# A four-stage transformer block on one core: how layers hand over, two orders changed, the output in parts

## The reference

```python
x = x + 0.5 * L0_ffn(layernorm(x))    # 8 experts, top 2, for each of gate, up, down
x = x + L0_attn(layernorm(x))         # 16 heads of 8; weights polymax(s), no softmax
x = x + 0.5 * L0_ffn(layernorm(x))
x = x + 0.5 * L1_ffn(layernorm(x))    # 128 -> 512 -> 128, gelu; weights of each batch element
x = x + L1_attn(layernorm(x))         # 16 heads on one latent of 36; softmax
x = x + 0.5 * L1_ffn(layernorm(x))
```

## Time and profile before

| what | us |
| --- | --- |
| median of 3 executions (lowest, highest) | 3112.09 (3107.85, 3112.73) |
| the profiled execution, its own time | 3102.54 |
| its span | 3100.8 |
| TensorE busy | 2719.5 (88 %) |
| VectorE busy | 2029.5 (65 %) |
| ScalarE busy | 1148.7 (37 %) |
| GpSimd busy | 884.5 (29 %) |
| landing of the 2 MB output | 8.7 |
| landing of an 8 KB row of maxima | 1.8 |
| landing of a 256 KB weight issued among many others | 5.4 |

### The profile page before, as it was taken

How to read it: one execution, slowest core, us unless ns; L and a number is a source line. 1 busy time by engine, 2 the same in 40 slices (tenths; PEclk the granted TensorE clock), 3 DMA queues, 4 the chain that set the end, 5 groups by cost and what they waited for, 6 DMA issues and landing times. The chain is left out here.

```text
span 3100.8 us, 53905 instructions
## 1 busy us (share of the span) xinstructions
PE 2719.5 (88%) x15208; PEld 1879.4 (61%) x15208; DVE 2029.5 (65%) x5166; ACT 1148.7 (37%) x2097; POOL 884.5 (29%) x1200
## 2 busy tenths in 40 slices
PE   6999999958787888789999999768988989889986
PEld 5888888735454555468888887334554554454453
DVE  6777777747776777577777777445555555556533
ACT  3111111126575657521111111324544535545532
POOL 3333223225555555442233222001211111111200
PEclk9999999968888888889999999878999999999988
DMA  3000000000000000020000000000101101101100
GB/s 134 0 0 0 0 0 0 1 1 3 3 2 3 3 3 2 17 84 0 0 0 0 0 0 0 1 23 27 45 24 35 37 25 36 36 24 38 34 1 27
DMA packets 31864, 52.01 MB, mean 17 GB/s; under 512 B 8066, under 2 KB 13954, under 8 KB 31620
## 3 DMA queue, kind: packets, MB, share of 16 engines
q1 hardware_dynamic: 27012, 41.88, 4.3%
q0 software_dynamic: 4608, 7.09, 0.9%
HBM read 17.93 MB, written 2.10 MB: 6 GB/s over the span
## 5 line engine op out<-in xcount | busy, mean ns | idle before, releaser
L603 DVE SCALAR_TENSOR_TENSOR moe_acc<-moe_ps,moe_comb,moe_acc 128x512 f32<-128x512 f32 x896 | 660.4, 743 | 153.1 <-PE moe_ps L310 146.8
L2149 DVE CUSTOM_DVE_ANT_0 attn_masked<-attn_psm,attn_causal 128x256 f32<-128x256 f32 (+7 forms) x512 | 368.6, 756 | 271.3 <-PE attn_psm L1846 270.3
L2051 ACT ACTIVATE attn_probs<-attn_pse 128x512 f32<-128x512 f32 (+1 forms) x640 | 313.2, 556 | 324.9 <-PE attn_pse L1861 322.2
L310 PE MATMUL moe_ps<-moe_Wg,moe_xh 128*128 128x512 f32 x1024 | 328.1, 402 | 17.4 <-DVE moe_Wg L526 17.4
L341 PE MATMUL moe_ps<-moe_Wd,moe_ih 128*128 128x512 f32 x1024 | 339.3, 413 | 4.7 <-DVE moe_Wd L526 4.7
L310 PE MATMUL moe_ps<-moe_Wu,moe_xh 128*128 128x512 f32 x1024 | 332.0, 406 | 3.5 <-POOL moe_Wu L464 3.5
L1769 POOL TENSOR_SCALAR_AFFINE_SELECT attn_probs<-attn_probs 128x256 f32<-128x256 f32 (+1 forms) x192 | 95.0, 495 | 726.3 <-ACT attn_probs L2051 726.3
L1877 PE MATMUL attn_psy<-attn_probs,attn_V 128*64 128x512 f32 (+3 forms) x1536 | 288.7, 506 | 0.0
L474 POOL TENSOR_SCALAR moe_part<-consts,moe_pick,moe_prob 128x8 f32<-128x8 f32 x256 | 97.4, 394 | 626.0 <-ACT moe_prob L398 626.0
L1077 POOL TENSOR_TENSOR attn_R<-attn_R 128x1024 f32<-128x1024 f32 (+1 forms) x128 | 215.0, 1687 | 200.2 <-DVE attn_R L1421 200.1
L1846 PE MATMUL attn_psm<-attn_kS,attn_qS 108*128 108x512 f32 (+3 forms) x672 | 199.0, 397 | 45.7 <-DVE attn_mx L2149 39.7
(11 more groups left out here) (218 smaller groups left out, 4802.5 us busy)
## 6 DMA issues: line engine op xcount, KB each, us to landing
attn_qS<-attn_qH SPq DMA_DIRECT2D x192, 72.0 KB
attn_qS<-attn_qL SPq DMA_DIRECT2D x96, 72.0 KB
attn_qS<-attn_qH POOLq DMA_DIRECT2D x64, 72.0 KB, 2.0
moe_stageg<-in_w_gate SPq DMA_DIRECT2D x8, 512.0 KB, 7.1
moe_stageu<-in_w_up SPq DMA_DIRECT2D x8, 512.0 KB, 7.2
moe_stageg<-in_w_down SPq DMA_DIRECT2D x8, 512.0 KB, 4.4
attn_qS<-attn_qL POOLq DMA_DIRECT2D x32, 72.0 KB, 2.5
out<-X SPq DMA_DIRECT2D x1, 2048.0 KB, 8.7
```

The source lines that it names most:

```text
L310: last = pe.matmul(expert_bank[j % 4][:, :], a[q][:, :], w[b][:, cols], start=k == 0, stop=k == 2)
L603: dve.scalar_tensor_tensor(acc[:, q, r, :], expert_bank[j % 4][:, :], comb[:, q, r, e:e + 1], acc[:, q, r, :], ALU.mult, ALU.add).then_inc ...
L2051: act.activation(probs[:, ring(q, u), c, HALF - n:HALF], e_part(k, HALF - n, HALF), ACT.Exp, scale=SCORE_SCALE).then_inc(p_ready, 1)
L2149: dve.tensor_tensor_reduce(masked[:, 0 if j >= 4 else 1, 0:n], m_all[:, base:base + n], causal[:, SEQ - n:SEQ], 1.0, NEG, ALU.add, ALU.max ...
```

## The change

Semaphores of a phase are cleared by SyncE within the next one (`clear_spent`), behind SyncE's own first or last work there, and no block of their own is left; the last phase's are cleared in `end_phase`. An activation on one element asks for a table ahead of time: square root at the end of four phases and, without a switch, of polynomial attention (`load_sqrt`), gelu ahead of the feed-forward loop, exp ahead of latent attention's. `ffn_phase` can get an output; it then adds into X at once, without statistics, and SyncE sends X out by 4 tiles of tokens as each half is done. The orders in the two attentions change as the pieces below show.

```diff
+    def clear_spent(self, sp):
+        if self.spent:
+            for s in self.spent.all:
+                sp.sem_clear(s)
...
@@ ffn_phase, SyncE
+                def store(b):
+                    for s in range(2):
+                        n = b * BT + 4 * s
+                        sp.wait_ge(res.xo_ready, after(b * 2 + s))
+                        sp.dma_start(out.rearrange("(n p) c -> p n c", p=P)[:, n:n + 4, :], t.X[:, n:n + 4, :]).then_inc(out_done, 16)
+                rows(0)
+                sem.clear_spent(sp)
+                for b in range(BATCH):
+                    if b + 1 < BATCH:
+                        rows(b + 1)
+                    if out is not None:
+                        store(b)
@@ ffn_phase, ScalarE
                 layernorm_scales(act, t, rstd_ready)
+                act.activation(t.warm[:, :], t.consts[:, 0:1], ACT.Gelu)
...
+                load_sqrt(act, t)
@@ ffn_phase, VectorE
-                        res.add(dve, b * 2 + s, s, b * BT + 4 * s, x_bank[s][:, :])
+                        if out is None:
+                            res.add(dve, b * 2 + s, s, b * BT + 4 * s, x_bank[s][:, :])
+                        else:
+                            some = bass.ds(b * BT + 4 * s, 4)
+                            dve.tensor_tensor(t.X[:, some, :], x_bank[s].rearrange("p (j c) -> p j c", c=DIM), t.X[:, some, :],
+                                              ALU.add).then_inc(res.xo_ready, 1)
@@ attn0_phase, TensorE
+                def visible(q, s):
+                    for kt, at_, qc, n, _ in key_units(s)[0]:
+                        pe.matmul(y_bank[:, qc:qc + n], KV[q][:, kt, P:2 * P], seen_one[:, :], start=at_ == 0, stop=False,
+                                  skip_group_check=True)
...
+                    if u == NQ0:
+                        pe.wait_ge(yc_ready, after(m * 2))
+                        visible(q, 1)
...
+                def highest(m, g):
+                    pe.wait_ge(yc_ready, after(m * 2 - 1))
                     pe.wait_ge(bound_ready, after(m * 3 + 2))
-                    pe.matmul(a_bank[0:1, 0:GH], bound[:, g % 2, 2:3], head_mask, start=True, stop=True).then_inc(peak_ready, 1)
+                    pe.matmul(y_bank[0:1, 0:GH], bound[:, g % 2, 2:3], head_mask, start=True, stop=True).then_inc(peak_ready, 1)
...
+                        if k >= 2:
+                            values(m, g, k - 2)
+                        if k == 0:
+                            highest(m, g)
+                        if k == 1:
+                            pe.wait_ge(top_ready, after(m))
+                            visible(g % 2, 0)
...
-                        if k >= 2:
-                            values(m, g, k - 2)
-                        if k == 4:
-                            highest(m, g, has_next)
@@ attn1_phase
+        def max_part(n, lo, hi, spare):
+            other = spare and len(of_kind(n)) % 2 == 1
+            if IN_ORDER[n][1] >= 4:
+                return (y_all if other else m_all)[:, lo:hi]
+            return e_all[:, lo:hi] if other else m_all[:, 2 * HALF + lo:2 * HALF + hi]
...
+        OUT_ORDER = [4, 5, 6, 7, 0, 1, 2, 3]
...
+                        if k == 1 and i == 0:
+                            pe.wait_ge(res.xo_ready, after(b * BT - 1))
...
-                        pe.wait_ge(res.xo_ready, after(b * BT + BT - 1))
```

191 lines of the change are left out of this document (104 added, 87 removed).

## The result

| what | us |
| --- | --- |
| median of 4 executions (lowest, highest) | 3030.08 (3019.35, 3033.86) |
| the kernel before, beside it | 3109.97 (3106.03, 3112.73) |
| ratio, 95% interval | 0.9738 (0.9709 to 0.9768) |
| the profiled execution, its span | 3026.82, 3025.1 |

A forecast was written before the change was run, and what follows sets the result against it. Seven stages in sequence, each with its own limit and a barrier between, bound the kernel. Terms -19.0 - 0.4 - 12.6 - 6.0 - 10.2 - 11.3 + 6 = -53.5 us gave 3058.6 us, range 3038 to 3077.

The forecast's parts named there:

- Seams: Five stage openings: the clear block and four square root table loads go from 23.5 us of VectorE idle time; -19.0 us.
- Gelu and exp tables: Feed-forward and latent attention loops: loading ahead gains 0 for gelu (other end 7.7 us), 0.5 us for exp.
- Latent attention's opening: Reordered start 6.8 us sooner, second bank for 16 maxima 6.2 less, moved projection -0.4; sum -12.6 us.
- Latent attention's ends and exp: Ends of batch elements and loop turns: transposes 3.6, scores ahead of residual 1.9, with exp's table -6.0 us.
- Last feed-forward layer and end: Direct residual add and faster product -10.2 us, shorter add chain and split output -11.3; reordered primes -0.2 per feed-forward opening.
- Polynomial attention: Steps of 33.95 us: early `visible` and `values` first cost +0.8 in 12 steps, element ends -0.7 four times; +6 us.
- Polynomial attention gains too: Rival: its low-clock stretch shrinks or `values` first hides both waits; 16 us better than +6, total 3040; chance 0.18.
- the clock end: Polynomial attention's low end, -10 us: clock rises some 3 us sooner, -0.6 x 12 - 2.8.
- The openings move a wait only: Rival: maxima stay with DMA or TensorE, output transfers delay rows; loses 8 of 12.6, 6 of 10.2; 3073; chance 0.16.
- The clears don't vanish: Rival: clears on SyncE still delay the barriers, all five seams keep 3 us; 3074; chance 0.03.
- Slower: Rival: polynomial attention's low clock lasts longer in 15 steps; outweighs the gain from 3.6 us each, 3149 at 6; chance 0.03.
- What I said would prove me wrong: Polynomial attention's step under 33.5 us, maxima over 16 us, or the last layer's rows landing behind the transposes.

The follow-up runs named there:

- e: Changed kernel with each phase's semaphores cleared in a block of their own again; 3050.16 us, seams 19.4 us against 6.2.
- f: Changed kernel without the activations that load the square root's table at the end of a phase; 3033.26 us.
- g: Changed kernel without gelu's table asked for ahead of the feed-forward loops, so six loads again; 3034.43 us.
- i: Changed kernel with X sent out in one transfer behind the last barrier, direct add kept; 3036.12 us.
- j: Changed kernel with X sent out in one transfer and the last layer's residual through copy and statistics again; 3055.92 us.
- c: Changed kernel with `values` still ahead of `prepare`, but `visible` at the tail of each half and the peak at unit 4 again; 3029.36 us.
- y: Kernel before, with only `values` ahead of `prepare` and ScalarE's first-half copy ahead of its preparation and squares; 3099.08 us against 3107.53.
- b: Changed kernel with `values` behind `prepare` and ScalarE's first-half copy behind the squares again, peak and `visible` still early; 3036.69 us.
- k: Changed kernel with latent attention's opening in the old order, normalising still first, two banks kept; 3047.54 us in one execution.
- h: Changed kernel with latent attention's 16 first maxima over one pair of banks again; 3041.41 us.
- d: Changed kernel with polynomial attention's `visible` one unit later, ahead of the first values; 3044.16 us.
- l: Changed kernel with VectorE taking the peak and first half of the next keys ahead of unit 1's take in polynomial attention; 3017.49 us.
- m: c's kernel with VectorE taking the first half of the next keys ahead of unit 1's take, peak still late; 3026.01 us.
- l_again: The same file as l against the kernel before, measured again in five rounds; 3016.08 us, ratio 0.971.

## Why the prediction was wrong, point by point

- **Seams.** Forecast -19.0, measured -17.3: the parts are 13.2 for the clears (e) and 3.7 for the tables (f), for which I had counted four loads of 1.28, 5.1. I had left 1.5 us at the second mixture layer (1.4 measured) and 0.75 at the others; they are 1.7, 1.2, 0.6 and 1.2. Right in kind, 1.7 too much.
- **Gelu and exp tables.** 0 for gelu is right (g). The first feed-forward layer nevertheless gave 3.5 us, at a clock of 0.89 for 0.86. I had no term for it, and what sets it stays open: the same code came at 0.86 in three other kernels.
- **Latent attention's opening.** Forecast -12.6, measured -13.7 (50.57 to 36.90) in the first profiles and -16.2 in the second. The start came 6.5 us sooner for 6.8. The maxima's stage fell from 20.13 us to 12.86, not 13.9, with VectorE busy 11.20 of it: 1.0 us undersized. The time from there to the exponent's scores stayed (3.29 and 3.35 us), where I had taken 0.4 off for the moved projection.

```profile
2045.19:2058.05 12.86, 10.29 (x24) 6.60 (x25) 11.20 (x32) 0.00 (x0) 0.37 (x2) 0.51 0.25 72
```

- **Latent attention's ends and exp.** Forecast -6.0; what the layer gained beyond the opening is 7.7 us in the first profiles, 8.0 by the means. No run takes these edits out one by one, so the 2 us above the forecast stay unexplained.
- **Last feed-forward layer and end.** -10.2, -11.3 and -0.2 forecast, -22.7 measured in the first profiles. The product took 3.70 us in every turn of the changed kernel, as expected, for the 5.40 of the earlier trace rows, and the end is 2.8 us behind the last add, for the 3.3 in my sum. (Eight transfers one after another at the 2.4 us measured for each would end 17 us later than one, not 12; nothing in the sum used it.) How it splits was not quite as told: the output alone is 6.6 us (i), the add's chain in all turns and at the end 17.9 (j).
- **Polynomial attention: the step that failed.** "+0.8 us for a step whose next step follows, 12 times". The +0.8 was fine for the step that I had read (33.95 to 34.9). But the 12 steps are of four kinds, of 35, 45, 34 and 46 us, and I had read one. In the second kind, with the next element's normalising and transposes, the old order had three waits of 1.2 to 2.5 us with products at the low clock behind two of them; the new order keeps two of these waits but has less of the low clock there (a clock of 0.88 for 0.78 over the step shown, 11.1 us at the lower level for 16.5 by the means) and in the step after (3.2 us for 10.2). The shorter low stretch is measured; what makes it shorter is not, beyond that `values` ahead of `prepare` brings it (c, y). The layer's change is -12.8 by the means (-15.1 in the pair of first profiles), which is 19 us of the 24 us by which the sum was off; the rest is the first feed-forward layer (3.3), latent attention (4.4), the last stage (1.9) and the second mixture layer (0.7), less the seams (1.7) and the first mixture layer (3.7).
- **The rivals.** "Polynomial attention gains too" named the right mechanism, a shorter low-clock stretch, with -10 us as its end; I had the clock end at 0.6 us a step, and it was some 3 us in two of four steps. It was given 0.18, and even its 3040 us lies 10 above the measured time. Of the two waits that it named, the 0.65 us before the sum's product is gone (it comes back in b). "The openings move a wait only" fell: k and h show both edits paying, 6.8 and 7.25 us. "The clears don't vanish" fell with the seams. "Slower" fell too, but d shows that it was near: one edit in the same place cost 14 us.
- **What I said would prove me wrong** (a step under 33.5 us) did: 31.6 us in the third steps.

## What to carry to other kernels

Measure the length of every pass of a loop that does different work in different passes before one is multiplied by their number: a list of one marker's start times takes a minute and would have shown four kinds of step. Where TensorE's granted clock goes up and down within a loop, an edit's price is not its own time: add up the layer's TensorE busy time at the same count of matmuls, before and after, and look at its idle time apart from it. In the change itself and in d most of the difference stood in the busy time; in l and m the waiting fell by 7 to 16 us. And the operation that TensorE waits for belongs first on its engine, ahead of one that nobody waits for yet: 1.2 us moved gave 9 to 14 us.

## What the runs showed of the hardware

Three things that I had not expected. The granted clock of a layer with 4944 matmuls moved between 0.82 and 0.89 with the order of its instructions, and TensorE's busy time with it between 530.7 us (d) and 506.4 (l_again); nine profiles of one order differed by 0.02 and 10 us. Moving a product a unit later (d) made the stretch at the lower level 3.4 us longer in the step shown and cost 14 us in all, while c, with a like wait (2.08 us for 2.46) in the same empty gap, lost nothing. And a table load in a loop turn, six of them of 1.28 us, cost nothing at all in two layers, while at a seam three of four cost nearly their full length.
